# A gather-and-interpolate stage: two corners added on VectorE in every fourth chunk, three transposes in place of six on TensorE

## The reference, cut to what matters

```
lo = jnp.floor(pos).astype(jnp.int32)
hi = jnp.minimum(lo + 1, Ll - 1)
frac = pos - lo.astype(x.dtype)
g_lo = xh[b_ix, lo]
g_hi = xh[b_ix, hi]
g = g_lo + frac[..., None, None] * (g_hi - g_lo)
out_h = jnp.einsum('blshd,blhs->blhd', g, w)
```

## Time and profile before

| | |
|---|---|
| time, median of 3 runs | 1921.41 us (1919.87 to 1926.05) |
| the profiled execution | 1925.06 us, span 1923.0 us |
| mean granted TensorE clock | 0.914 of full speed |
| busy share of the span | PE 81%, DVE 65%, POOL 58%, ACT 51% |
| POOL's first and last gather begin at | 329.3 and 1830.8 us |

### The profile page before, as it was taken

One profiled execution on the slowest core, in us unless ns is written; L12 is line 12 of the kernel. 1 busy time (PEld: TensorE's weight loads), 2 busy tenths in 40 slices (PEclk: granted clock), 3 DMA queues, 4 the chain that ended last, 5 costly groups with the idle time before them and its releaser, 6 DMA issues.

```text
span 1923.0 us, 31790 instructions
## 1 busy us (share of the span) xinstructions
PE 1557.4 (81%) x12145; PEld 1060.6 (55%) x12153; DVE 1252.3 (65%) x2158; ACT 976.3 (51%) x2359; POOL 1110.5 (58%) x1069
## 2 busy tenths in 40 slices
PE   4688787878798978788979777879897689899866
PEld 3355454546565645465656454656574367677535
DVE  6665563678776855797768557977685454354345
ACT  3266566535546564255465651655556344444333
POOL 0000001777776757777777467777774777777700
PEclk8899999989998988999989888999899899899866
DMA  4010002434433434334334343344343633333311
GB/s 163 1 29 17 15 21 43 110 99 118 116 112 96 119 80 119 101 110 120 112 100 119 75 121 101 109 114 117 103 119 76 180 110 102 105 99 103 103 20 44
DMA packets 93421, 178.74 MB, mean 93 GB/s; under 512 B 21452, under 2 KB 50264, under 8 KB 93016
## 3 DMA queue, kind: packets, MB, share of 16 engines
q0 software_dynamic: 50688, 138.48, 26.3%
q1 hardware_dynamic: 42584, 38.23, 7.1%
HBM read 151.46 MB, written 9.44 MB: 84 GB/s over the span
## 4 chain that ended last, share of the span: by engine, by line
PE 49%; DVE 15%; ACT 13%; POOL 11%; issue 7%; DMA 3%; SPq 1%; DVEq 0%; ACTq 0%; POOLq 0%
POOL pool_c L746 11%; PE c L1630 7%; ACT prob L877 3%; PE sc L1605 2%; PE ta L1560 2%; ACT pool_a L788 2%; PE pa L1526 2%; DVE pool_c L1253 2%; PE pb L1526 2%; DMA pool_c<-rows_of_x,idx 2%; PE c L1526 2%; PE ta L1534 2%; PE tb L1407 2%; PE tb L1534 2%; DVE ssq L1150 2%
## 5 line engine op out<-in xcount | busy, mean ns | idle before, releaser
L746 POOL DMA_INDIRECT pool_c<-rows_of_x,idx x1056 | 1107.6, 1049 | 720.7 <-DVE pool_c L1341 325.8
L1253 DVE TENSOR_TENSOR pool_c<-pool_c 128x768 f32<-128x768 f32 x352 | 332.2, 951 | 124.5 <-DMA pool_c<-rows_of_x,idx 124.4
L1630 PE MATMUL c<-ident,pool_c 128*128 128x128 f32 x2112 | 310.8, 287 | 64.3 <-DVE pool_c L1253 64.2
L1630 PEld LDWEIGHTS c<-ident,pool_c 128*128 128x128 f32 x2112 | 255.1, 148 | 147.9 <-DVE pool_c L1253 83.2
L877 ACT ACTIVATE prob<-sc,nmax 128x128 f32<-128x128 f32 x512 | 179.3, 374 | 0.2
L788 ACT COPY pool_a<-tb 128x512 f32<-128x512 f32 x188 | 114.3, 608 | 11.9 <-PE tb L1407 6.3
L877 ACT ACTIVATION_READ_ACCUMULATOR prob<-sc,nmax 128x1 f32 x512 | 109.9, 215 | 0.0
L1150 DVE TENSOR_REDUCE ssq<-pool_a 128x16 f32<-128x1024 f32 x64 | 77.8, 1216 | 38.1 <-ACT pool_a L853 37.6
L1560 PE MATMUL ta<-vmix,pool_a 128*64 128x64 f32 x1024 | 71.9, 224 | 27.6 <-ACT pool_a L788 27.6
L1560 PEld LDWEIGHTS ta<-vmix,pool_a 128*64 128x64 f32 x1024 | 64.5, 138 | 48.0 <-issue 48.0
L1160 DVE TENSOR_REDUCE nmax<-sc 128x8 f32<-128x1024 f32 x64 | 76.7, 1198 | 14.3 <-PE sc L1605 14.2
(11 more groups left out here) (461 smaller groups left out, 3251.8 us busy)
## 6 DMA issues: line engine op xcount, KB each, us to landing
pool_c<-rows_of_x,idx POOLq DMA_INDIRECT x1056
vmix<-vring SPq DMA_DIRECT2D x128, 128.0 KB
rows_of_x<-x2tok SPq DMA_DIRECT2D x16, 256.0 KB
xtok<-in_x SPq DMA_DIRECT2D x4, 512.0 KB, 6.7
x_of_all<-x2tok SPq DMA_DIRECT2D x8, 256.0 KB, 2.8
out<-pool_c SPq DMA_DIRECT2D x8, 256.0 KB, 2.3
wqkv<-in_wqkv SPq DMA_DIRECT2D x1, 1536.0 KB
xtok<-x_of_all SPq DMA_DIRECT2D x3, 512.0 KB, 4.7
```

The lines of the kernel that those rows point to most:

```text
L746: pool.indirect_dma_start(gat[:, n % GB, s, :], None, tables[b % 2], bass.IndirectOffsetOnAxis(ap=idx[:, t, SC * c + s:SC * c + s + 1], ax ...
L1253: V.tensor_tensor(g4, g4, wv, ALU.mult).then_inc(SEM["c_prod"], 1)
L1630: ins = mm(out[:, c:c + P], x, ident[:], start=(i == 0 and k == 0), stop=(i == BCH - 1 and k == len(parts) - 1), is_transpose=True, skip_g ...
```

## The change

In the chunks n with n % 4 == 2 (2, 6, ..., 86, so 22 in each batch and 88 in all) DVE does a second instruction. It waits for its own product through a new semaphore `c_pair`, adds the upper corner's 3 x 128 values to the lower corner's, and only then raises `c_prod`. PE turns the three sums there and not the six pieces. The other chunks, the gathers, the buffers and every engine's order of steps stay as they are; the lists of times are not changed.

```
+PAIRED = tuple(n for n in range(CHUNKS) if n % 4 == 2)
...
-            ... "c_prod": CHUNKS, "c_acc": CHUNKS - J,
+            ... "c_prod": CHUNKS, "c_pair": len(PAIRED), "c_acc": CHUNKS - J,
...
-                    V.tensor_tensor(g4, g4, wv, ALU.mult).then_inc(SEM["c_prod"], 1)
+                    ins = V.tensor_tensor(g4, g4, wv, ALU.mult)
+                    if n in PAIRED:
+                        ins.then_inc(SEM["c_pair"], 1)
+                        wait(dve, "c_pair", b, PAIRED.index(n) + 1)
+                        rows = gat[:, n % GB]
+                        V.tensor_tensor(rows[:, :, 0:D], rows[:, :, 0:D], rows[:, :, D:2 * D], ALU.add).then_inc(SEM["c_prod"], 1)
+                    else:
+                        ins.then_inc(SEM["c_prod"], 1)
...
-                    parts = [gat[:, n % GB, s, D * h:D * (h + 1)] for s in range(SC) for h in range(2)]
+                    parts = [gat[:, n % GB, s, D * h:D * (h + 1)] for s in range(SC) for h in range(1 if n in PAIRED else 2)]
```

More of the change, by code:

```diff
@@ L518, in build @@
             "b_max": 16, "b_recip": 16, "b_mix0": 256, "b_mix1": 256, "b_newton": 48, "c_newton": 8, "f_shift": 9, "f_edge": 1, "f_hn": 4, "f_res": 2,
-            "c_silu": 2, "c_act": 4, "c_pos": 2 * POS, "c_w": T, "c_table0": 48, "c_table1": 48, "c_prod": CHUNKS, "c_acc": CHUNKS - J,
+            "c_silu": 2, "c_act": 4, "c_pos": 2 * POS, "c_w": T, "c_table0": 48, "c_table1": 48, "c_prod": CHUNKS, "c_pair": len(PAIRED), "c_acc": CHUNKS - J,
             **{f"c_gather{i}": 16 * SC * -(-(CHUNKS - i) // GB) for i in range(GB)},
```

## The result

The changed kernel takes 1932.38 us (median of 8 runs, 1928.72 to 1936.34), the kernel before, run beside it, 1921.72 (median of 8, 1918.32 to 1928.73). The ratio is 1.0046 with a 95% interval of 1.0028 to 1.0064: 8.8 us slower, between 5.4 and 12.3. The time lies in the range of the prediction and on its slower side; the forecast of +2.8 us, no measurable change, was too low.

What follows compares the result with a forecast made beforehand. POOL was taken to bound the tail and first halves, PE, DVE and ACT streams the second halves. Terms +2.3, +2.4 and -1.9 us sum to +2.8, forecasting 1924.2 us; the range holding 8 in 10 was 1913 to 1936.

Steps and rivals of the forecast that it cites:

- The sum, +2.8 us: Whole kernel: tail +2.3, first halves +2.4 and second halves -1.9 us make +2.8 us, no measurable change.
- Three kinds of stretch: POOL sets the end in the tail and first halves; PE, DVE and ACT streams do in three second halves.
- The prices: Paired chunks: add 555 ns, 0.03 us behind its product; a gather starting into it held until 0.82 us after its end.
- The tail, +2.3 us: Batch 3's chunks: POOL sets the end, PE's savings are worth nothing, adds hold gathers; +2.3 us, bounds 0 and 9.5.
- Five clear holds and half of four on the edge: Tail's 22 adds: five hold a gather 0.2 to 0.4 us (1.5 us), half of four edge cases add 0.8 us.
- The first halves, +2.4 us: Batches 0 to 2 up to about chunk 40: POOL sets pace, held gathers cost 1.0, 0.3 and 1.1 us.
- DVE's 6.3 us of waiting: First halves: DVE waits 6.3 us for gathers, into which the adds' 4.7 us a batch fit.
- The second halves, -1.9 us: Chunks 46 to 86, batches 0 to 2: PE's savings less DVE delays give -0.6 us a batch, -1.9 in all.
- the tile: Attention tile of 11.5 us in second halves: add fills DVE's 0.52 us idling, DVE sets pace, +0.07 us each.
- Every add holds a gather: Rival, slower: two thirds of 46 adds in POOL's stretches cost 0.43 us each, giving 1932.5 us; chance 0.2.
- DVE becomes the second halves' pace: Rival, slower: half of 33 adds land on the path, +9.7 us plus 4.7 of held gathers, 1935.8; chance 0.13.
- PE's saving counts: Rival, faster: second halves give up to -10.9 us, ending near 1913 with 3 us of held gathers; chance 0.2.

Runs made afterwards that it cites:

- e3: Changed kernel with a small one-input DVE reduction between product and add, so adds begin 0.25 us later; ratio 1.0056 against the kernel before.
- e9: Kernel before with only chunks 2 to 42 of batches 0 to 2 paired; ratio 1.0021, +4.0 us.
- e6: Kernel before with only the last batch's 22 chunks paired; ratio 1.0019, +3.7 us.
- e10: Kernel before with 17 chunks of each of batches 0 to 2 paired, chosen where DVE idles behind their product; ratio 0.9999, -0.2 us.
- e11: Kernel before with PE turning only three pieces in chunks 46 to 86 of batches 0 to 2, no adds, upper corners left out; ratio 0.9976, -4.6 us.
- e12: Kernel before with PE turning three pieces in chunks 46, 54, 62, 82, 86 of batches 0 to 2, no adds; ratio 0.9924, -14.6 us.
- e8: Kernel before with only chunks 46 to 86 of batches 0 to 2 paired, 33 in all; ratio 0.9989, -2.1 us.
- e7_five: Kernel before with only chunks 46, 54, 62, 82, 86 of batches 0 to 2 paired; ratio 0.9950, 1914.14 us.
- e7_again: Kernel before with only chunks 46, 54, 62, 82, 86 of batches 0 to 2 paired, on another chip; ratio 0.9953, 1913.62 us.

## Why the prediction was right, and where it was not

**The sum, +2.8 us:** 6.0 too low. The parts run alone make +5.6; the tail and the first halves are 1.4 and 1.6 us above their forecasts there, each inside its interval, and the other 3.2 us of the change's 8.8 are in no part. So the sum was short, and which term is to blame is not shown.

**Three kinds of stretch:** right as far as it shows. The parts, run alone, come out with the signs that were given them; the intervals of the tail and of the second halves include no change.

**The prices:** 0.56 us for an add, 0.03 us behind its product, and a gather held until 0.82 us behind the add's end are what the profile after shows.

**The tail, +2.3 us:** right in cause: eight adds hold a gather, for 2.6 us, and none does in e3. Five clear holds and half of four on the edge were counted. That the length grew by just 2.3 (350.2 - 347.9) is partly luck, since it moves by more than that in kernels with no add there.

**The first halves, +2.4 us:** right in kind, perhaps too small. The profile has +6.3, the timed e9 +4.0 (1.0 to 6.9). The working counted gathers that an add itself holds: in the profile after there are five, with 1.5 us, in e9's nine, with 2.5. The gathers there grew by 4.4 us, but in the nine kernels with no add in the first halves they take 377.5 to 380.9 us, so the 378.1 of before is at the low end. The adds also push the products and the two-input steps behind them 0.59 us along, and these may hold other gathers than before, which the working left out when it took DVE's 6.3 us of waiting for cover; no run isolates that. The 1.9 us at POOL's wait ahead of chunk 7 may be scatter: that wait is 3.5 and 6.2 us in profiles of kernels with nothing paired in the first halves (e6 in batch 2, e10 in batch 1). The working was also uneven: chunks 10 to 42 have nine adds a batch, where its bound counts eight, and the adds of chunks 2 and 6 stand in no term. In the profile after none of these six holds a gather.

**The second halves, -1.9 us:** -2.1 timed and -1.1 in the profile, so nothing speaks against the size; but three such halves move by 5 us with nothing paired. In the tile the mechanism is as told, DVE's idle time is used up and it sets the pace; its room was read too small (11.43 us, forecast 11.62). The price under it was not as steady as it looked: 0.33 us a sum on PE's path gave 24 x 0.33 = 7.9 us for e11, which is the very edge of what was measured, and 5 for e12, which gained 14.6. The prediction read clock and PE time together from one execution, as though the time at the lower clock would stay as it was.

**The rivals.** *Every add holds a gather* gave 1932.5, where the time came out, but by luck: eight of 22 adds hold one in the tail, 2.6 us and not 9.5, and five in the first halves. *DVE becomes the second halves' pace*: in the attention tiles yes, for the time no (e8). *PE's saving counts*: not in the change, where the adds of other places outweigh it; but chosen chunks alone make it true, at 1914.

## What to carry to other kernels

A trade of engine time is decided stretch by stretch: the same edit cost some 4 us in the first halves and 2 to 4 in the tail, where gathers set the pace, and gave 9 in five chunks of each of three second halves. Before a term of a few us is read off two profiles, look how far that stretch moves in profiles of kernels whose edit does not touch it. When taking work from TensorE, compare its granted clock by stretch before trusting a price for each instruction.

## What the runs showed of the hardware

- Whether a VectorE instruction with two inputs in SBUF slows a POOL gather depends on which begins first, with an edge near 0.046 us: 113 gathers that began 0.047 us or more into an add all ended some 0.82 us behind it, two of them 0.91 (one that met an add 0.05 us old took 1.33 us); of 45 that began at most 0.045 us into one, 43 took their 0.95 and two 1.05; and an add that began 0.20 us inside a gather left both at their 0.95 and 0.56.
- After the same 2.0 us wait at the same step TensorE's granted clock over the next 5 us was 0.67 in one execution of a program and 1.00 in another (e7_five and e7_again).
- In nine second halves with the same instructions, each us at the lower clock went with 0.41 us of length.
